# Top-2 mixture stage: column-tile work gathered into one run per chunk, router tiles and the helpers' order moved

## The reference

```python
t = t + ffn(layer_norm(t))          # D = C = 64, E = 8, K = 2
router_probs = softmax(x @ router_w + router_b)
top_p, top_i = top_k(router_probs, 2)
top_p = top_p / sum(top_p)
expert_out = einsum('bnd,edc->bnec', x, expert_w) + expert_b
out = einsum('bnk,bnkc->bnc', top_p, gathered(expert_out, top_i))
```

## Time and profile before

| what | value |
|---|---|
| median of the runs | 2475.13 us |
| the profiled execution's own time | 2466.83 us |
| its span | 2465.0 us |
| instructions | 37697 |
| PE busy | 2093.9 us (85%) |
| DVE busy | 1505.6 us (61%) |
| ACT busy | 1041.1 us (42%) |
| POOL busy | 576.2 us (23%) |
| mean granted TensorE clock | 0.961 |

### The profile page before, as it was taken

How to read it: one execution, slowest core, us unless ns; L and a number is a source line. 1 busy time by engine, 2 the same in 40 slices (tenths; PEclk the granted TensorE clock), 3 DMA queues, 4 the chain that set the end, 5 groups by cost and what they waited for, 6 DMA issues and landing times. The chain is left out here.

```text
span 2465.0 us, 37697 instructions
## 1 busy us (share of the span) xinstructions
PE 2093.9 (85%) x12605; PEld 1537.3 (62%) x12605; DVE 1505.6 (61%) x3011; ACT 1041.1 (42%) x2868; POOL 576.2 (23%) x630
## 2 busy tenths in 40 slices
PE   5999952799999968877877787777887699999999
PEld 2555522577777757777767777677777455555554
DVE  4666678355555544444444444444444699999998
ACT  3666632133333313333344444444444544454442
POOL 3555512022112200000000000000000656665562
PEclk9999985699999989999999999999999799999999
DMA  3855520122222200000000000000000455555543
GB/s 90 232 170 161 170 72 9 52 86 86 86 86 86 74 15 0 0 0 0 0 3 0 0 0 0 0 0 0 0 0 0 114 134 127 131 133 129 133 118 79
DMA packets 176418, 159.05 MB, mean 65 GB/s; under 512 B 25976, under 2 KB 126360, under 8 KB 176280
## 3 DMA queue, kind: packets, MB, share of 16 engines
q1 hardware_dynamic: 175768, 156.91, 23.2%
q0 software_dynamic: 512, 0.53, 0.1%
HBM read 56.72 MB, written 67.11 MB: 50 GB/s over the span
## 5 line engine op out<-in xcount | busy, mean ns | idle before, releaser
L1091 PE MATMUL s_ps<-g_yh,g_Tlo 128*128 128x256 f32 x1905 | 336.1, 307 | 211.3 <-DVE g_yh L1119 195.4
L1091 PEld LDWEIGHTS s_ps<-g_yh,g_Tlo 128*128 128x128 f32 x1905 | 256.5, 190 | 289.9 <-DVE g_yh L1119 273.4
L1165 ACT ACTIVATE g_X<-s_xs 128x256 f32<-128x256 f32 x254 | 177.6, 699 | 382.2 <-DVE g_yl L1109 382.2
L1457 POOL TENSOR_TENSOR g_X<-tm_x,g_X 128x512 f32<-128x512 f32 x64 | 83.4, 1322 | 1051.6 <-DVE tm_m L1537 1051.6
L1119 DVE SCALAR_TENSOR_TENSOR g_yh<-s_ps,s_xs 128x256 fp32r<-128x256 f32 x254 | 107.9, 425 | 354.3 <-PE s_ps L1095 354.3
L1546 DVE TENSOR_TENSOR tm_Z<-tm_pg,tm_nd 128x1024 f32<-128x1024 f32 x256 | 299.0, 1209 | 10.7 <-PE tm_pg L1340 10.5
L1095 PE MATMUL s_ps<-g_yl,g_Thi 128*128 128x256 f32 x1905 | 293.1, 284 | 0.0
L1091 PE MATMUL s_ps<-g_yh,g_Thi 128*128 128x256 f32 x1905 | 292.3, 284 | 0.0
L1095 PEld LDWEIGHTS s_ps<-g_yl,g_Thi 128*128 128x128 f32 x1905 | 258.2, 190 | 0.0
L1091 PEld LDWEIGHTS s_ps<-g_yh,g_Thi 128*128 128x128 f32 x1905 | 255.4, 189 | 0.0
L1352 PE MATMUL tm_po<-tm_Z,g_wexp 128*64 128x512 f32 x1024 | 247.7, 605 | 0.0
(11 more groups left out here) (284 smaller groups left out, 3871.2 us busy)
## 6 DMA issues: line engine op xcount, KB each, us to landing
tm_nd<-tm_nS SPq DMA_DIRECT2D x256, 128.0 KB, 2.3
g_X<-in_x SPq DMA_DIRECT2D x128, 128.0 KB, 3.0
x1s<-g_X SPq DMA_DIRECT2D x64, 256.0 KB, 2.1
x1tok<-g_X SPq DMA_DIRECT2D x64, 256.0 KB, 2.8
tm_x<-x2s SPq DMA_DIRECT2D x64, 256.0 KB, 2.9
y<-tm_yo SPq DMA_DIRECT2D x128, 128.0 KB, 2.5
g_X<-x1s SPq DMA_DIRECT2D x32, 256.0 KB, 2.8
x2s<-g_X SPq DMA_DIRECT2D x32, 256.0 KB, 2.0
```

Source lines behind the costliest of these rows:

```text
L1091: pe.matmul(out, t[:, d * P:d * P + P], g.yh[:, :, d:d + 64], start=(t is g.Tlo[i] and d == 0), stop=False)
L1165: act.activation(line(*place(n)), xs[n % RING][:], ACT.Copy).then_inc(stored, 1)
```

## The change

- **PE.** A step now has two halves i instead of four parts. In each, the four `experts` calls of a chunk run in one piece on the column tiles, and everything on the full array runs in one piece before them: broadcasts q, q + 1; router tiles; broadcast q + 2; `centre(t, i)`; broadcast q + 3; `biases`; `turn_gates`. The first two broadcasts of a step no longer come at the end of the step before. The router tiles go half a step later: `tiles(t, 0)` into the second half of step t, `tiles(t, 1)` into the first half of step t + 1.
- **ACT.** `read_tiles(t - 1, 1)` and `rstd(t - 1)` go from the end of step t - 1 to the start of step t, with `copy_centred(t, 0)` between them; `read_tiles(t, 0)` goes behind the exponential.
- **POOL.** The order in a step was `scale`, `split`, `low_part(t, 1)`, `x3` twice, `low_part(t + 1, 0)`, `weigh`. It becomes `x3(t + 1, 0)`, `scale`, `low_part(t, 1)`, `split`, `x3(t + 1, 1)`, `low_part(t + 1, 0)`, `weigh`.
- **DVE.** Four products in a run instead of two; then `y_of`; then in the first half c11, c12, c0 to c4, in the second half c5 to c10. Before, two products lay between c12 and c0.

No instruction is added or taken away, no buffer is changed, and the order of the DMA queue stays.

```diff
--- before.py
+++ after.py
@@ -1355,25 +1355,29 @@
 
                 for t in range(STEPS):
                     near, ex = t - 2, t - 3
-                    for p in range(EP):
-                        if now(t) and p % 2 == 1:
-                            tiles(t, p // 2)
-                        if now(ex) and p % 2 == 0:
-                            biases(ex, p // 2)
-                        for q in (2 * p + 2, 2 * p + 3):
-                            if q < UNITS and now(ex):
-                                broadcast(ex, q)
-                            if q >= UNITS and now(near):
-                                broadcast(near, q - UNITS)
-                        if now(t) and p % 2 == 0:
-                            centre(t, p // 2)
-                        if now(ex) and p == 0:
+                    for i in range(2):
+                        q = i * EP
+                        if now(ex):
+                            broadcast(ex, q)
+                            broadcast(ex, q + 1)
+                        if i == 0 and now(t - 1):
+                            tiles(t - 1, 1)
+                        if i == 1 and now(t):
+                            tiles(t, 0)
+                        if now(ex):
+                            broadcast(ex, q + 2)
+                        if now(t):
+                            centre(t, i)
+                        if now(ex):
+                            broadcast(ex, q + 3)
+                            biases(ex, i)
+                        if i == 0 and now(ex):
                             turn_gates(ex, 1, 2 * t)
-                        if now(near) and p == 2:
+                        if i == 1 and now(near):
                             turn_gates(near, 0, 2 * t + 1)
                         if now(ex):
-                            experts(ex, 2 * p)
-                            experts(ex, 2 * p + 1)
+                            for ep in range(EP):
+                                experts(ex, q + ep)
 
             @block.scalar
             def _(act):
@@ -1429,25 +1433,26 @@
                 high_part(0, 0)
                 for t in range(STEPS):
                     near, ex = t - 2, t - 3
+                    if now(t - 1):
+                        read_tiles(t - 1, 1)
                     if now(t):
                         copy_centred(t, 0)
+                    if now(t - 1):
+                        rstd(t - 1)
                     if now(ex):
                         copy_gates(ex, 1)
                     if now(t):
                         high_part(t, 1)
-                        read_tiles(t, 0)
                     if now(t - 1):
                         wait(act, s["shifted"], t)
                         act.activation(EX[:], L[:], ACT.Exp).then_inc(s["exp"], 1)
                     if now(t):
+                        read_tiles(t, 0)
                         copy_centred(t, 1)
                     if now(near):
                         copy_gates(near, 0)
                     if now(t + 1):
                         high_part(t + 1, 0)
-                    if now(t):
-                        read_tiles(t, 1)
-                        rstd(t)
 
             @block.gpsimd
             def _(pool):
@@ -1497,14 +1502,15 @@
                 low_part(0, 0)
                 x3(0, 1)
                 for t in range(STEPS):
+                    if now(t + 1):
+                        x3(t + 1, 0)
                     if now(t - 1):
                         scale(t - 1)
+                    if now(t):
+                        low_part(t, 1)
                     if now(t - 2):
                         split(t - 2)
-                    if now(t):
-                        low_part(t, 1)
                     if now(t + 1):
-                        x3(t + 1, 0)
                         x3(t + 1, 1)
                         low_part(t + 1, 0)
                     if now(t - 1):
@@ -1607,23 +1613,23 @@
                         dve.reciprocal(total[:], total[:]).then_inc(s["inverse"], 1)
 
 
-                slots = [(), (0, 1, 2, 3, 4), (5, 6), (7, 8, 9, 10)]
+                slots = [(0, 1, 2, 3, 4), (5, 6, 7, 8, 9, 10)]
 
                 for t in range(STEPS):
-                    for p in range(EP):
+                    for i in range(2):
                         if now(t - 3):
-                            z_of(t - 3, 2 * p)
-                            z_of(t - 3, 2 * p + 1)
-                        if now(t - 4) and p == 0:
+                            for ep in range(EP):
+                                z_of(t - 3, i * EP + ep)
+                        if i == 0 and now(t - 4):
                             y_of(t - 4, 1)
-                        if now(t - 2) and p == 0:
+                        if i == 1 and now(t - 3):
+                            y_of(t - 3, 0)
+                        if i == 0 and now(t - 2):
                             choose(t - 2, 11)
                             choose(t - 2, 12)
                         if now(t - 1):
-                            for n in slots[p]:
+                            for n in slots[i]:
                                 choose(t - 1, n)
-                        if now(t - 3) and p == 2:
-                            y_of(t - 3, 0)
 
 
 class Shared:
```

## The result

The changed kernel takes 2620.36 us (median of four runs, 2618.15 to 2626.72) beside 2474.27 us for the kernel before: the ratio is 1.0595, with a 95% interval of 1.0573 to 1.0617. It is slower by 146 us; 2620 was predicted. The profiled execution shows a span of 2616.3 us.

What follows compares the result with a forecast made beforehand. PE sets the 16.21 us step, with DVE close behind at 16.0. From 2475 us, 94 for c4's wait and hold plus 3.4 at the ends give 97, the clock 48: 2620 us, range 2545 to 2650.

Steps and rivals of the forecast that it cites:

- The step that decides: c4: DVE, first half step: c4 waits for POOL's split until 9.9 us; with its hold, steps grow 3.2 us, 96 in all.
- The hold of c4 by the addition: DVE's c4 starts behind POOL's addition and ends only after it, at 11.3 us; 1.1 us per step.
- The low part in front of the split: POOL, first half step: low part runs 5.46 to 6.73 us, split follows until 9.86.
- The clock: PE idles 3.2 us per step, so its granted clock halves: +1.7 us in 28 steps, 48 us.
- rival 1: PE's clock holds in the mixture; c4's wait costs the same, idle time nothing: 2572 us, chance 0.27.
- Rivals 2 and 3: DVE's c4: a lighter wait, 2514 us, chance 0.13; or no wait, not slower, 2472 us, chance 0.02.
- Rival 4: PE's clock stays low twice as long, 3.4 us in 28 steps: 2667 us, chance 0.08.
- The saved switches: PE saves one column-tile round trip per half, 0.34 us; only 0.2 of 0.68 us per step can show.
- The step if nothing waits: DVE's reordered instructions in the steady mixture take 16.1 us per step without waits.
- The ends: Last two steps: PE's order of four shows, 7.5 us per half against 6.65, +3 us; start-up +0.4.

Runs made afterwards that it cites:

- split-first run: Changed kernel with POOL's split put back before the low part: 2571.53 us, ratio 1.0406.
- the run without holds: Changed kernel with two F1 buffers, biases before centring, old PE order from step 32, split before low part, `high_part(t + 1, 0)` before centred copy: 2481.63 us.
- the run in which the clock holds: Changed kernel with the first two broadcasts of the second half step issued three times each: 2575.69 us, ratio 1.0427.

## Why the prediction was right

- **The step that decides: c4.** Right in place and size. The layout from the earlier trace rows gave 9.9 for c4 and 11.3 for the second half, measured 9.85 and 11.13. The run with two buffers shows that this wait is the cause, and the old kernel with c0 to c4 moved shows that it needs nothing else of the change.
- **The hold of c4 by the addition.** Predicted 1.1 us from one instance in the start-up; the early additions give 1.07.
- **The low part in front of the split.** Predicted at 0.9 to 1; 0.96 by the split-first run, between c12 and c4.
- **The clock.** Predicted 1.7 us per step, 48 us; filling PE's idle time gives back 1.50 per step, 45 us in all. The two levels and the 3.2 us of idle time came from the earlier trace rows and the layout; 2.71 us of idle were measured. With rival 1 (the clock holds) the time would have been 2572; the run in which it was made to hold took 2575.69. Rivals 2 and 3 fall with c4's 2.23 us in every step. Rival 4 falls too: the 29 low stretches in steps 3 to 32 last 109.2 us together, and only three of them were twice as long as the others. That a fall had to come in nearly every step was taken from one row with 2.86 us of idle time; the runs with 1.67 to 1.75 us, in which it came in 16, 18 and 26 of 30 steps, show that with a gap one microsecond shorter it isn't sure.
- **The saved switches.** This term was mis-sized. I had PE's own need fall by 0.34 us a half, from 8.11 to 7.77; in the run without holds, in which PE is never idle, it is 8.16: 0.15 saved in the run of four pairs, where I had 0.23, and 0.20 lost in the full-array work, where I had 0.11 saved. That nothing of the saving would show in the step was right, but partly by luck, since there was none, and DVE's 16.0 us, my reason, was not what hid it.
- **The step if nothing waits.** The 16.1 us failed: with c4's wait gone it is 16.71. What the runs showed in its place is two limits close together. At 16.71 PE sets the step, with centring behind the reading of `bankA`, which I had called free. With that mended DVE sets it at 16.47, with c1, c2, c4 and c5 held by POOL for some 2.2 us together, where I had priced c4's hold alone. In the changed kernel itself this cost little, since the second half came out at the 8.1 us that I took (19.23 less 11.13, by the run in which the clock holds).
- **The ends.** +3 predicted, +7.9 measured. The term was mis-sized: I left out the turning of gates (0.5 us in a half, as in the steady step) and that the clock falls there too. A half at the full clock takes 8.09 us, where I had 7.5; the two halves of steps 33 and 34 with a low stretch take 9.7 and 9.8.
- That the total met the measurement within 1 us is partly two errors that cancel: the steps 3 to 32 were 7 us over, the ends 5 us under.

By the rule that the prediction names (the Trainium skill, TensorE: Matmul & The Clock Gate, HAM oscillation — how this bites in real kernels) the price of the low clock is paid anew at each burst after a wait. The trace of the changed kernel agrees: 0.50 once in nearly every step, and none when the gap was filled. The run with early additions agrees in half of its steps only, 16 of 30.

## What to carry to other kernels

When instructions are regrouped for one engine, list for every wait what stood between its producer and its consumer before and what stands there afterwards: here c12 and c4 stood 4.02 us apart, of which two products were 2.2, and the split on another engine needs 3.45 of them, so that without the products the cover falls short. No row of the steady part showed the wait; one of the start-up did. A start-up or tail, where such cover is missing, is the place to read the prices from. And an engine that isn't late itself can still be made slow by the idle time given to it: price the clock together with the wait, and test it by filling the gap with harmless work.

## What the runs showed of the hardware that was not expected

- TensorE's clock fell to 1.2 GHz after idle stretches of 1.7 us (the old kernel with c0 to c4 moved, 26 stretches in steps 3 to 32), not only after the 2.86 us of the earlier trace rows; with the stretch filled, so that 0.88 us were left, it did not fall in any of the 30 steps. Between the two it is open: after 1.67 us in the run with early additions it fell in 16 steps of 30 and stayed up in the others.
- A DVE instruction with two inputs in SBUF that starts while POOL works on its own inputs ended about 0.15 us behind POOL's instruction in each instance read, whatever its own length: 1.36 or 0.29 us for the same c4. It goes the other way too: in the run with two buffers for F1 the split's third instruction took 0.77 us beside c4, which started with it, and 0.61 in the changed kernel. The cost moves to another instruction with each shift of the order: c4 (1.36), c1 (1.00) and c7 (1.38) in the changed kernel, c1, c4 and c5 in the run with the old order at the end, none of c1, c4, c5 and c7 beyond 0.46 us in the run that moved `high_part` too.
